# A graph network on one Trainium2 core: moving the odd ninth tile of the weighted sums to round one, beside the fix columns, with six wider strip slots in place of seven

## What is computed

```python
def _gcn_conv(x, row, col, ew, W, b, n_nodes):
    xw = x @ W
    deg = jax.ops.segment_sum(ew, col, num_segments=n_nodes)
    dinv = jnp.where(deg > 0, jax.lax.rsqrt(deg), 0.0)
    norm = dinv[row] * ew * dinv[col]
    msg = xw[row] * norm[:, None]
    out = jax.ops.segment_sum(msg, col, num_segments=n_nodes)
    return out + b
...
h = _gcn_conv(x, row, col, ew, W1, b1, n)   # then relu
h = _gcn_conv(h, row, col, ew, W2, b2, n)   # then relu
h = _gcn_conv(h, row, col, ew, W3, b3, n)
...
x = _layernorm(x + _L3_gnn_ref(...), axis=-1)
```

## Time and profile before

| | us |
|---|---|
| median of 3 runs | 6155.77 |
| lowest and highest | 6154.3, 6158.61 |
| the profiled execution | 6162.13 |
| its span | 6160.3 |
| PE busy | 3501.4 (57%) |
| DVE busy | 2947.6 (48%) |
| ACT busy | 1698.5 (28%) |
| POOL busy | 3305.7 (54%) |

### The profile page before, as it was taken

The page is one execution under the profiler, slowest core; times in us unless marked ns, Lnnn a source line. Parts: engine busy times, 40 slices in busy tenths (PEclk is TensorE's granted clock), DMA queues, the critical chain, the costliest instruction groups (busy, mean ns, idle before and its releaser), DMA issues. The chain is left out here.

```text
span 6160.3 us, 43118 instructions
## 1 busy us (share of the span) xinstructions
PE 3501.4 (57%) x13009; PEld 2058.1 (33%) x13009; DVE 2947.6 (48%) x6440; ACT 1698.5 (28%) x2011; POOL 3305.7 (54%) x3349
## 2 busy tenths in 40 slices
PE   3000000050097789999999211111099999999999
PEld 2000000010043347777777100010054445444544
DVE  4766666678666664556564455555560000000111
ACT  2443343121010005666677333333340000000000
POOL 5777777577777777777775677777610000000000
PEclk7555555575598899999999555555599999999999
DMA  5566565399953443444578333333478888888887
GB/s 146 191 221 219 210 224 199 102 365 367 338 175 99 134 131 111 113 116 125 139 227 251 102 122 111 111 122 111 129 233 284 295 295 296 291 295 300 291 302 259
DMA packets 509068, 1255.65 MB, mean 204 GB/s; under 512 B 114558, under 2 KB 164196, under 8 KB 500132
## 3 DMA queue, kind: packets, MB, share of 16 engines
q1 hardware_dynamic: 387860, 1126.44, 54.0%
q0 software_dynamic: 119952, 125.65, 8.5%
q10 hardware_dynamic: 1024, 0.79, 0.0%
HBM read 873.83 MB, written 378.71 MB: 203 GB/s over the span
## 5 line engine op out<-in xcount | busy, mean ns | idle before, releaser
L838 POOL DMA_INDIRECT plane<-total,cell x1568 | 1617.6, 1032 | 491.5 <-issue 425.3
L470 POOL DMA_INDIRECT gb<-rows,src x1564 | 1486.3, 950 | 526.5 <-issue 475.2
L1014 PE MATMUL psum<-gb,big 128*128 128x512 f32 (+1 forms) x3822 | 1585.4, 569 | 3.0 <-DVE turned L1198 2.4
L1014 PEld LDWEIGHTS psum<-gb,big 128*128 128x128 f32 x3822 | 695.1, 191 | 765.8 <-issue 764.8
L1412 PE MATMUL psum<-gb,row_part 128*128 128x512 f16 x1911 | 420.5, 374 | 476.4 <-DMA gb<-plane 476.4
L2486 ACT COPY gb<-turned 128x1632 f32<-128x1632 f32 (+3 forms) x138 | 450.9, 3267 | 722.8 <-DVE turned L2581 722.8
L1412 PE MATMUL psum<-strips,ring 128*128 128x512 f32 (+1 forms) x2548 | 611.3, 395 | 13.5 <-issue 7.5
L2507 PE MATMUL psum<-identity,end_top 128*8 128x128 f32 (+1 forms) x2 | 0.8, 376 | 1084.7 <-DVE end_top L2587 1084.7
L1432 ACT CAST strips<-gb 128x1024 fp32r<-128x1024 f16 (+1 forms) x529 | 559.6, 1075 | 131.5 <-DMA gb<-plane 40.0
L2875 PE MATMUL psum<-w_L_gnn_skip_W,turned 128*128 128x128 f32 x98 | 39.0, 502 | 847.1 <-ACT turned L2893 847.1
L2581 DVE TENSOR_TENSOR_SCAN turned<-gb,psum 128x1632 f32<-128x1632 f32 (+3 forms) x138 | 457.8, 3317 | 68.8 <-ACT gb L2468 66.2
(11 more groups left out here) (423 smaller groups left out, 4665.7 us busy)
## 6 DMA issues: line engine op xcount, KB each, us to landing
gb<-plane SPq DMA_DIRECT2D x588, 512.0 KB, 4.4
gb<-plane SPq DMA_DIRECT2D x294, 576.0 KB, 4.8
plane<-turned SPq DMA_DIRECT2D x49, 3200.0 KB, 28.4
gb<-plane SPq DMA_DIRECT2D x588, 256.0 KB, 3.1
gb<-plane SPq DMA_DIRECT2D x294, 288.0 KB, 3.3
plane<-turned SPq DMA_DIRECT2D x49, 1600.0 KB
runs<-gb SPq DMA_DIRECT2D x33, 1748.0 KB, 6.1
runs<-gb SPq DMA_DIRECT2D x33, 1610.0 KB, 5.7
```

Source lines behind the costliest of these rows:

```text
L470: m.s_rows[b % BUFS].up(nc.gpsimd.indirect_dma_start(m.batch(b, columns, row)[:, j, 0:width], None, table, bass.IndirectOffsetOnAxis(ap=m. ...
L838: done.up(m.nc.gpsimd.indirect_dma_start(plane, bass.IndirectOffsetOnAxis(ap=m.cell[:, r:r + 1], axis=0), total[:, r:r + 1], None), 16)
L1014: mm = nc.tensor.matmul(m.psum[:, self.bank(r, 0, i), 0:nodes], rows, slot[:, a:a + nodes], start=(s == 0), stop=False)
```

## The change

The weighted sums get rounds of their own, (9, 8, 8, 8, 8, 8). Round zero's first quad holds one tile alone, tile 0; its columns lie in the plane right behind the fix columns, and one product of 256 columns takes both, in bank 0. The fix product of that tile goes to columns 256 to 384 of the same bank, and VectorE scales the two parts apart and adds them: three instructions of 128 columns. A slot grows to 10 x 128 columns, and there are six. In round zero of the first layer VectorE adds to strips 4 and 5 behind quad 0, to 6 and 7 behind quad 1 (then the marks, for nine tiles), and to strip 8 behind quad 2. The sums over counted edges (`CountSums`), a subclass, keep the old rounds by overrides. Place and size of the other buffers stay.

```diff
-SLOTS, SLOT = 7, max(ROUNDS) * P
+SLOT = max(ROUNDS) * P
+PLANE_ROUNDS = (9, 8, 8, 8, 8, 8)
...
+SLOTS, PLANE_SLOT, SPOT_AT = 6, P + max(PLANE_ROUNDS) * P, 7 * SLOT
...
+def plane_quads_of(r):
+
+    before = sum(-(-size // QUAD) for size in PLANE_ROUNDS[:r])
+    a, b = sum(PLANE_ROUNDS[:r]), sum(PLANE_ROUNDS[:r + 1])
+    odd = (b - a) % QUAD
+    assert odd in ((0,) if r else (1,))
+    starts = ([a] if odd else []) + list(range(a + odd, b, QUAD))
+    return [(before + i, i, range(t, n)) for i, (t, n) in enumerate(zip(starts, starts[1:] + [b]))]
...
     def slot(self, n):
-        return self.m.gb[:, n % SLOTS * SLOT:(n % SLOTS + 1) * SLOT]
+        return self.m.gb[:, n % SLOTS * PLANE_SLOT:(n % SLOTS + 1) * PLANE_SLOT]
...
-        for _, i, tiles in quads_of(r):
-            nodes = len(tiles) * P
-            a = fixed + i * QUAD * P
-            mm = nc.tensor.matmul(m.psum[:, self.bank(r, 0, i), 0:nodes], rows, slot[:, a:a + nodes], start=(s == 0), stop=False)
-        if r == 0:
-            mm = nc.tensor.matmul(m.psum[:, 2, 0:P], rows, slot[:, 0:P], start=(s == 0), stop=(s == TILES - 1))
+        for _, i, tiles in self.quads_of(r):
+            place = self.place_of(r, tiles)
+            if self.beside_fix(r, i):
+                mm = nc.tensor.matmul(m.psum[:, self.bank(r, 0, i), 0:2 * P], rows, slot[:, 0:2 * P], start=(s == 0), stop=(s == TILES - 1))
+            else:
+                mm = nc.tensor.matmul(m.psum[:, self.bank(r, 0, i), 0:len(tiles) * P], rows, slot[:, fixed + place.start:fixed + place.stop],
+                                      start=(s == 0), stop=False)
         m.s_used.up(mm)
 
+    def beside_fix(self, r, i):
+
+        return r == 0 and i == 0
...
+            apart = self.beside_fix(r, i)
+            to = slice(2 * P, 3 * P) if apart else slice(0, len(tiles) * P)
...
+        if self.beside_fix(r, i):
+            c = Chain(dve, m.s_chain)
+            sums, fixes = (m.psum[:, self.bank(r, 0, i), k * P:(k + 1) * P] for k in (1, 2))
+            c.start(m.nc.vector.tensor_tensor(sums, sums, factors, ALU.mult))
+            c.link(m.nc.vector.tensor_tensor(out, fixes, factors, ALU.mult))
+            c.wait()
+            m.s_drained.up(m.nc.vector.tensor_tensor(out, sums, out, ALU.add))
+        else:
+            m.s_drained.up(m.nc.vector.tensor_tensor(out, sums, factors, ALU.mult))
...
                 elif g == 1:
-                    for n in range(SLOTS, ROUNDS[0]):
+                    for n in range(SLOTS, SLOTS + 2):
                         sums.add_own(dve, n)
                     sums.mark(dve, 0)
+                elif g == 2:
+                    for n in range(SLOTS + 2, sums.rounds[0]):
+                        sums.add_own(dve, n)
```

More of the change, by code:

```diff
@@ L928, in __init__, with quads_of, quads_by, place_of @@
         self.data = m.s_drained if factors is None else m.s_biased
+    rounds = PLANE_ROUNDS
+    def quads_of(self, r):
+        return plane_quads_of(r)
+    def quads_by(self, r):
+        return sum(len(self.quads_of(n)) for n in range(r + 1))
+    def place_of(self, r, tiles):
+        a = (tiles[0] - sum(self.rounds[:r])) * P
+        return slice(a, a + len(tiles) * P)
     def at(self, signal, n):
@@ L975, in sp @@
             wait_cells(m, sp, self.n)
-        for r in range(len(ROUNDS)):
+        for r in range(len(self.rounds)):
             a, b = self.columns(r)
@@ L1005, in step @@
         if r == 0 and self.after:
-            for g, i, tiles in (quad for n in range(len(ROUNDS)) for quad in quads_of(n)):
+            for g, i, tiles in (quad for n in range(len(self.rounds)) for quad in self.quads_of(n)):
                 if s == tiles[0]:
@@ L1034, in add_own @@
         r, s = divmod(n, TILES)
-        a = (s - sum(ROUNDS[:r])) * P + (0 if r else P)
+        a = (s - sum(self.rounds[:r])) * P + (0 if r else P)
         cells = self.strip(n)[:, a:a + P]
@@ L1123, in pe @@
     def pe(self, pe):
-        for r in range(len(ROUNDS)):
-            other, before = (self, r - 1) if r else (self.after, len(ROUNDS) - 1)
-            parts = len(quads_of(before)) * other.parts if other else 0
+        for r in range(len(self.rounds)):
+            other, before = (self, r - 1) if r else (self.after, len(self.rounds) - 1)
+            parts = len(other.quads_of(before)) * other.parts if other else 0
             if r == 0 and self.tail:
@@ L1144, in last_net @@
     def last_net(self, pe):
-        r = len(ROUNDS) - 1
-        for at in range(len(quads_of(r)) * self.parts):
+        r = len(self.rounds) - 1
+        for at in range(len(self.quads_of(r)) * self.parts):
             self.net(pe, r, at)
@@ L1170, in act @@
         if self.result is not None:
-            for g, i, tiles in quads_of(len(ROUNDS) - 1):
+            for g, i, tiles in self.quads_of(len(self.rounds) - 1):
                 self.root(act, g, tiles)
@@ L1346, in sp @@
         if not self.after:
-            for r in range(len(ROUNDS) - 1):
-                t = sum(ROUNDS[:r + 1])
+            for r in range(len(self.rounds) - 1):
+                t = sum(self.rounds[:r + 1])
                 needs.append(sp.value_load(m.need[P - 1:P, t - 1:t], min_val=1, max_val=EPOCHS))
@@ L1586, in deviations @@
         c = Chain(dve, m.s_chain)
-        t = slice(sum(ROUNDS[:r]), sum(ROUNDS[:r + 1]))
+        t = slice(sum(self.rounds[:r]), sum(self.rounds[:r + 1]))
         c.wait()
@@ L1669, in net_before @@
     at, beyond = divmod(s - sums.lag(r), 5)
-    if beyond != 4 or before is None or not 0 <= at < len(quads_of(old)) * before.parts:
+    if beyond != 4 or before is None or not 0 <= at < len(before.quads_of(old)) * before.parts:
         return None
@@ L1850, in _ @@
             scale(sums, last)
-            for at in range(len(quads_of(last))):
+            for at in range(len(sums.quads_of(last))):
                 take(sums, how, last, at)
```

106 lines of the change are left out of this document (55 added, 51 removed).

## The result

The changed kernel takes 6170.64 us (median of 17 runs, 6164.63 to 6177.64) where the kernel before takes 6158.95 (17 runs, 6154.3 to 6163.54): a ratio of 1.002, with a 95% interval from 1.0013 to 1.0026. It is 11.7 us slower by the medians, and as the interval lies wholly above 1, the loss is real, though small. The forecast was +8.4 us and 6164.

The account below looks back on a forecast made before the run. TensorE was taken as the bound. Round one -10.9, 256-column product -0.9, tail +16.0 and seams +4.2 sum to +8.4 us: 6170.5 from the profiled 6162.13, or 6164 us as median; range 6154 to 6172.

Parts of the forecast that it names:

- the rival of the clock: Rival at the seams between layers: TensorE's longer idle time drops the granted clock, losing 1.8 to 3.4 us each; chance 0.11.
- Round one narrower: Round one of layer 1: its third product is dropped in 49 steps, taking 10.9 us away.
- The product of 256 columns: Layers 2 and 3: one 256-column pair at 0.435 us replaces two 128-column pairs at 0.444, 0.9 us less.
- The rival of the weight loads: Rival on TensorE: 128-column pairs are paid by weight loads, so a 256-column pair costs 0.222 us; total 6134 us; chance 0.03.
- The tail: Round zero of layer 1, beside the attention layer's end: +16.0 us, bounds 14 to 18.7.
- Step (a): Start of layer 1's round zero: VectorE's diagonal adds wait for larger strips 0 to 3, so all begins 0.4 us later.
- Step (b): Round zero of layer 1: strip 7 is requested one step later, VectorE waits, quad 1's transposes come 3.5 us later.
- Step (c): Round zero of layer 1: VectorE waits over 6 us for strip 8, quad 2's transposes come 8.3 us later.
- Step (d): Rest of layer 1's round zero: TensorE bound, 43 wider steps add 9.2 us, idle pieces absorb 1.5 us.
- The seams: Between layers: strip 3 is requested one step later and is larger, so the first matmul starts 2.1 us later per seam.
- Six slots in steady rounds: Steady rounds: a strip has 8.59 us from request to use and takes 4.4 us, so one slot fewer costs nothing.
- The tail has room: Rival in layer 1's round zero: quads, not TensorE, set the pace and catch up the late start; 6152 us; chance 0.08.

Follow-up runs that it names:

- six_narrow: The kernel before with six slots of its own width in place of seven, old rounds and products kept: 6170.09 us, ratio 1.0013.
- seven_wide: The changed kernel with a seventh wide slot in an array of its own: 6159.07 us, ratio 0.9994.
- late_add: The changed kernel with VectorE's add to strip 8 moved from behind quad 2 to behind quad 3 of the tail: 6168.17 us, ratio 1.0012.
- scale_first: The changed kernel with VectorE scaling the old layer's quads ahead of the add to strip 3 at the seams: 6167.85 us, ratio 1.0007.
- seven_scale_first: The changed kernel with seven wide slots and the scalings ahead of strip 3's add at the seams: 7087.51 us on the slower chip, ratio 1.0019.

## Why the prediction was right, and where its sizes were off

The verdict (a change of under 0.2%, on the slow side) and the mechanisms held. It held narrowly: the ratio of 1.002 lies on that bound, and 6170.64 us lies above the forecast's own range of 6159 to 6169. It is inside the 6154 to 6172 only by the part that was added for the rival of the clock, which had a chance of 0.11 and came true in part. The sum was 8.4 us and the measured difference of the stretches 10.9. Its terms in turn:

- **Round one narrower,** -10.9: measured -11.2, of which 0.3 is a fix product that moved to the end of round zero, where it costs the same. Right.
- **The product of 256 columns,** a pair 0.435 us between bounds of 0.222 and 0.859. Round zero of layer 2 went from 96.92 to 107.13 us, 0.208 a step more than with one pair of 128, so a pair is 0.430. The -0.9 us of layers 2 and 3 was -1.5. Right. The rival of the weight loads is refuted with it: 191 ns loads in the costliest group hold up no matmul. The Trainium skill's sentence that weight loads overlap running matmuls only where the row groups differ (TensorE: Matmul & The Clock Gate, section The mechanism) disagrees with the trace. The same section also lets a load go ahead into a background weight buffer, and that the trace doesn't contradict.
- **The tail,** +16.0: measured +17.3. Step (a), a start 0.4 us later, came as 0.5. Step (b), quad 1's transposes +3.5, came as +3.4. Step (c) put the wait for strip 8 near 4490 at over 6 us, quad 3's joining at 4495.6 and quad 2's transposes at 4501.7; measured in the same frame are 4489.3 + 4.6 with 6.17 us of wait, 4495.4 and 4501.4, so +8.0 for +8.3. Step (d) failed by 1.6 us (9.3 in place of 7.7): it followed TensorE from there by columns alone and left out that the late quad opens a second idle piece (3.92 us) ahead of those transposes. The clock fell again behind it, for 1.6 us, which the earlier trace rows had already shown behind the first. The columns came to 8.9 us for 9.2, and the moved fix product added 0.3. The total stayed inside the stated bounds of 14 to 18.7.
- **The seams,** +2.1 each: measured +2.45 and +2.15, with landings of 6.22 and 5.93 us for 5.9 and gaps of 3.66 and 3.37 us for 3.3. Right.
- **The clock at the seams** was a rival with a chance of 0.11, priced at 1.8 to 3.4 us a seam. It happened at one of two seams, both times the changed kernel was profiled, at 1.6 us. No row or run shows the price's upper end, 6.8 us of work at half speed: a fall cost 1.5 to 1.7 us, twice 2.9. The mechanism was given away too cheaply: of the stretch I read a low piece behind 8.57 us of idle time and none behind 1.21 us, and took the gap in between for the kind that does no harm, with no row for it. The rows were there, ahead of the stretch in the same trace of the kernel before. TensorE's timeline and the stretch behind it:

```profile
3082.60 0.76 PE L1412 MATMUL psum<-strips,high 128*128 128x512 f32 x2 [2.21 <-ACT strips L1432]
```

```profile
3083.20:3086.50 3.30, 3.30 (x12) 2.72 (x10) 3.30 (x6) 3.27 (x5) 2.69 (x3) 0.50 0.67 192
```

The same happened there behind 2.25 us (at 3216.28) and 2.20 us (at 3270.06). The Trainium skill's warning that waits for data between bursts put TensorE back to the low level (TensorE: Matmul & The Clock Gate, section HAM oscillation), which the prediction cited for this rival, is borne out by the 9 falls at the seams, but not as "each time": behind 3.46 and 3.66 us the clock stayed at 1.00.
- **Six slots in steady rounds,** 0: right, 85.90 us a round in six_narrow and the changed kernel.
- **The tail has room** (6152): refuted. In seven_wide, without the wait for strip 8, round one still starts later by about all the columns, 10.3 us for 10.2.

The level of the forecast was off by more than its difference. I took 6.4 us between the profiled execution and the median of three runs for a rule, but the median of 17 runs is 6158.95, 3.2 us above that of three. Of the 6.6 us between 6164 and 6170.64, 3.2 are the base and 3.3 the change (8.4 forecast, 11.7 by medians). Three runs that lie 4 us apart can't carry a base to better than that.

As for the cause: six_narrow shows that one slot fewer costs 10.5 us without any other edit, and seven_wide that the moved tile with seven slots costs 0.3. The whole-kernel times agree: six_narrow is slower, with an interval above 1 (1.0004 to 1.0023), and seven_wide can't be told from the kernel before (0.9985 to 1.0004). Two parts of that cost are shown apart: the wait for strip 8 by late_add (4.4 us, by one profile, in a tail that scatters by as much) and the wait ahead of the scalings by scale_first (4.2 us and the clock's 1.6). In the tail late_add leaves 2.6 us over seven_wide, which is not shown apart; VectorE's longer waits for strips 6 and 7 are the likely cause. Open remains what decides the clock between gaps of some 1.7 and 3.7 us.

## What to carry to other kernels

A slot less in a ring can leave every steady round untouched and still cost at each place where the consumer's engine does something else in the same queue: look for instructions that stand in order behind one that waits for a strip, ask whether they need it, and put them ahead (here a changed order alone took the seams from 2.5 and 2.2 us to 0.3 and 0.1). When an idle piece on TensorE grows from one to some 2 to 4 us, add the low clock behind it to the sum as a likely cost of 1.5 to 2.9 us, in a tail as well as at a seam, and look for gaps of that length in the whole trace, not only in the stage that changes. Compare profiles from the first instruction of the changed stage, not by their spans.

## What the runs showed of the hardware

- **The granted clock behind short idle time.** Over the 28 seams in the table it never fell behind 1.72 us or less (17 gaps, 0.84 to 1.72 us) and fell behind 1.83, 2.87, 3.01, 3.19, 3.29, 3.37, 3.60, 4.77 and 4.86 us. Behind 3.46 and 3.66 us it stayed at 1.00, so the length of the gap alone does not decide. A fall cost 1.5 to 1.7 us, twice 2.9. With products of no use in the gap the clock stayed up at both seams of one profile. Nor is a gap under 1.8 us safe: in an earlier stage of seven_scale_first it fell behind 1.68 us, with dense matmuls on both sides, while in seven_wide, in another such stage, it stayed up behind 2.67 us. TensorE's timelines, each with the stretch behind its gap:

```profile
3301.91 6.33 PE L1464 MATMUL psum<-strips,ring 128*128 128x512 f32 x23 [1.68 <-DVE ring L1499]
```

```profile
3302.80:3306.10 3.30, 3.30 (x11) 2.69 (x10) 0.77 (x3) 1.28 (x3) 2.59 (x3) 0.50 0.57 170
```

```profile
3079.66 0.73 PE L1464 MATMUL psum<-strips,high 128*128 128x512 f32 x2 [2.67 <-ACT strips L1484]
```

```profile
3080.00:3083.40 3.40, 3.40 (x19) 2.91 (x18) 3.40 (x8) 3.40 (x5) 2.63 (x3) 1.00 0.66 202
```

- **Landings at a seam.** A strip of 640 KB takes 5.0 us at the median, but 6.22 and 5.93 us as the fourth of a new layer, while a strip's use still frees a slot each 1.72 us.
- **Two chips.** On one the same kernel takes some 7070 us and not 6159. The weighted sums are alike there to 3 or 4 us (1724.6 and 1720.7 us before, 1734.8 and 1731.6 after), and all the rest of the difference stands ahead of them.
